# Query projections of a four-layer cross-attention kernel: one fp32 matmul against three bf16 products

## The reference, cut to what matters

```python
x      # (32, 56, 128)
ctx    # (32, 1500, 64)
# every layer, for each of 16 heads:
q = norm(x) @ Wq ; k = ctx @ Wk ; v = ctx @ Wv
x = x + softmax(q k^T * scale) v @ Wo
x = x + ffn(norm(x))       # experts, int8-like product, Fourier product, self-attention + MLPs
```

## Time and profile before

| | |
|---|---|
| median of three runs | 4396.57 us (4387.61 to 4402.43) |
| profiled execution, its span | 4385.4 us |
| what lies around the span, to the median | 11.17 us |
| TensorE busy | 4003.2 us, 91% |
| vector engine busy | 3408.8 us, 78% |
| scalar engine busy | 2756.6 us, 63% |
| GpSimd busy | 2685.0 us, 61% |
| mean granted TensorE clock | 0.939 |

### The profile page before, as it was taken

One profiled execution on the slowest core, in us unless ns is written; L12 is line 12 of the kernel. 1 busy time (PEld: TensorE's weight loads), 2 busy tenths in 40 slices (PEclk: granted clock), 3 DMA queues, 4 the chain that ended last, 5 costly groups with the idle time before them and its releaser, 6 DMA issues. The chain is left out here.

```text
span 4385.4 us, 103422 instructions
## 1 busy us (share of the span) xinstructions
PE 4003.2 (91%) x40427; PEld 2873.2 (66%) x40427; DVE 3408.8 (78%) x6672; ACT 2756.6 (63%) x5342; POOL 2685.0 (61%) x2445
## 2 busy tenths in 40 slices
PE   6999999888879999999799999996996899999977
PEld 4777777754545777777467777774664577777753
DVE  6999998667788888888688888876555888888833
ACT  4787877554446777777377777761441677777721
POOL 3888888656664767777367677771002476767730
PEclk9999999889989999999699999995997999999986
DMA  4333333124341111111111111100001111111100
GB/s 112 94 90 96 87 99 89 53 62 119 117 118 43 51 40 51 49 46 30 33 41 46 53 37 54 44 23 19 1 1 32 45 46 46 46 54 42 34 12 9
DMA packets 113025, 237.08 MB, mean 54 GB/s; under 512 B 15000, under 2 KB 53160, under 8 KB 111160
## 3 DMA queue, kind: packets, MB, share of 16 engines
q1 hardware_dynamic: 112088, 230.40, 18.3%
q10 hardware_dynamic: 448, 0.06, 0.0%
HBM read 165.23 MB, written 50.26 MB: 49 GB/s over the span
## 5 line engine op out<-in xcount | busy, mean ns | idle before, releaser
L483 POOL TENSOR_TENSOR wst<-wst 125x384 bf16<-125x384 f32 (+1 forms) x1536 | 1631.5, 1062 | 841.3 <-ACT wst L681 776.7
L681 ACT ACTIVATE wst<-ps 125x448 f32<-125x448 f32 x3072 | 1498.1, 543 | 406.9 <-PE ps L164 397.9
L738 DVE TENSOR_TENSOR wst<-wst 125x512 bf16<-125x512 f32 (+1 forms) x1536 | 1403.9, 915 | 270.5 <-ACT wst L681 254.9
L164 PE MATMUL ps<-big,cx 128*125 128x448 bf16 (+1 forms) x6144 | 1435.1, 355 | 0.0
L164 PEld LDWEIGHTS ps<-cx,wst 125*128 125x128 bf16 x23040 | 1105.4, 98 | 354.7 <-issue 60.2
L164 PE MATMUL ps<-cx,wst 125*128 125x65 bf16 (+2 forms) x23040 | 1202.3, 204 | 27.8 <-POOL wst L483 13.3
L164 PEld LDWEIGHTS ps<-big,cx 128*125 128x125 bf16 (+1 forms) x6144 | 814.6, 137 | 287.2 <-issue 23.1
L164 PE MATMUL ps<-cx,big 128*128 128x500 bf16 (+1 forms) x2688 | 713.2, 318 | 27.7 <-DVE wst L708 14.2
L705 DVE CUSTOM_DVE_ANT_0 wst<-ps,wst 128x500 bf16<-128x500 f32 x896 | 603.8, 674 | 166.3 <-PE ps L164 122.5
L630 ACT ACTIVATE wst<-ps 128x500 bf16<-128x500 f32 x896 | 530.1, 592 | 226.9 <-PE ps L164 173.5
L708 DVE TENSOR_REDUCE wst<-ps 128x1 f32<-128x500 f32 x896 | 600.5, 670 | 36.3 <-PE ps L164 27.1
(11 more groups left out here) (213 smaller groups left out, 4158.2 us busy)
## 6 DMA issues: line engine op xcount, KB each, us to landing
cx<-ctxT SPq DMA_DIRECT2D x96, 375.0 KB, 3.5
cx<-ctxN SPq DMA_DIRECT2D x64, 377.9 KB
cx<-in_ctxN SPq DMA_DIRECT2D x64, 375.0 KB
cx<-ctxT SPq DMA_DIRECT2D x96, 187.5 KB, 3.8
ctxN<-cx SPq DMA_DIRECT2D x32, 377.9 KB
ynN<-cx SPq DMA_DIRECT2D x32, 377.9 KB
cx<-ynN SPq DMA_DIRECT2D x32, 377.9 KB
cTs<-in_ctxT SPq DMA_DIRECT2D x64, 187.5 KB, 6.8
```

The source lines that it names most:

```text
L164: return t.matmul(o, l, r, start=start, stop=stop, skip_group_check=True)
L483: g.tensor_tensor(pl[r][0:KP, at:], pf[r][0:KP, at:], pf[r][0:KP, at:].bitcast(BF16)[:, 1::2], ALU.subtract).then_inc(s["plp"], 1)
L681: e.activation(pf[T % 3][0:KP, cols], bank(2 + n2 % 3, 448)[0:KP], ACT.Exp, scale=scale).then_inc(s["ev"], 1)
L738: v.tensor_tensor(pl[r][0:KP, 0:to], pf[r][0:KP, 0:to], pf[r][0:KP, 0:to].bitcast(BF16)[:, 1::2], ALU.subtract).then_inc(s["pl"], 1)
```

## The change

The projection becomes a sum of three bf16 products. Both operands are written as an upper bf16 half and the bf16 remainder: `xTh` and `xTl` in place of the turned activations, `wah` and `wal` beside the folded weights. The product of the two remainders is left out.

```diff
+            def project(o, g, c):
+                mm(t, o, wah2[:, g, :], tok8(xh_, c), True, False)
+                mm(t, o, wah2[:, g, :], tok8(xl_, c), False, False)
+                mm(t, o, wal2[:, g, :], tok8(xh_, c), False, True).then_inc(s["pm"], 1)
...
-                mm(t, bank((1 + g) % 8, 448), wa2[:, g, :], tok8(qsrc, 0), True, True).then_inc(s["pm"], 1)
+                project(bank((1 + g) % 8, 448), g, 0)
...
-                    mm(t, bank(7, 448), wa2[:, k, :], tok8(qsrc, p), True, True).then_inc(s["pm"], 1)
+                    project(bank(7, 448), k, p)
```

```diff
+        def act_turned_high(e, w, n):
+            for g4 in range(4):
+                w.wait_ge(s["tr"], 4 * n + g4 + 1)
+                e.activation(xTh[:, 512 * g4:512 * g4 + 512], bank(g4), ACT.Copy).then_inc(s["xTa"], 1)
+
+        def dve_turned_low(v, w, n):
+            for g4 in range(4):
+                cols = slice(512 * g4, 512 * g4 + 512)
+                w.wait_ge(s["xTa"], TURNED[n] - 3 + g4)
+                v.tensor_tensor(xTl[:, cols], bank(g4), xTh[:, cols], ALU.subtract).then_inc(s["xTd"], 1)
```

The folded weights. In layer 0 the scalar engine writes `wah` from PSUM and the vector engine `wal` from PSUM. In layers 1 and 2 the scalar engine writes `wa` and `wah`, and GpSimd subtracts. In the last layer (fold 4) both halves are made from `wa`, and the turned activations get theirs from `xT`:

```diff
+                if f == 4:
+                    w.wait_ge(s["f1d"], FOLD_D[3] + j + 1)
+                    e.activation(wah[:, 512 * j:512 * j + 512], wa[:, 512 * j:512 * j + 512], ACT.Copy).then_inc(s["f1a"], 1)
+                    continue
...
+                if f != 3:
+                    e.activation(wah[:, 512 * j:512 * j + 512], bank(4 + j), ACT.Copy).then_inc(s["f1a"], 1)
...
+        def pool_weights_low(g, w, f):
+            for j in range(2):
+                cols = slice(512 * j, 512 * j + 512)
+                w.wait_ge(s["f1a"], FOLD_A[f])
+                g.tensor_tensor(wal[:, cols], wa[:, cols], wah[:, cols], ALU.subtract).then_inc(s["wl"], 1)
+                w.wait_ge(s["wl"], FOLD_W[f] - 1 + j)
...
+            for g4 in range(4):
+                cols = slice(512 * g4, 512 * g4 + 512)
+                w.wait_ge(s["x3h"], g4 + 1)
+                g.tensor_tensor(x3l[:, cols], xT[:, cols], x3h[:, cols], ALU.subtract).then_inc(s["x3l"], 1)
+                w.wait_ge(s["x3l"], g4 + 1)
+            pool_weights_low(g, w, 4)
...
+            for g4 in range(4):
+                cols = slice(512 * g4, 512 * g4 + 512)
+                w.wait_ge(s["xTf"], 13 + g4)
+                e.activation(x3h[:, cols], xT[:, cols], ACT.Copy).then_inc(s["x3h"], 1)
```

More of the change, by code:

```diff
@@ L73, in build @@
         wav = wa[:, :].rearrange("p (h n) -> p h n", h=H)
-        wa2 = wa[:, 0:1024].rearrange("p (g n) -> p g n", g=H // 2)
+        wah, wal = (wa[:, 1024 + 512 * i:1536 + 512 * i].bitcast(BF16) for i in range(2))
+        wah2, wal2 = (v.rearrange("p (g n) -> p g n", g=H // 2) for v in (wah, wal))
+        xTh, xTl = (xT[:, 1024 * i:1024 * i + 1024].bitcast(BF16) for i in range(2))
         wbh = wb[:, 0:1024].bitcast(BF16)
@@ L192, in wait_turned @@
         def wait_turned(w, n):
-            w.wait_ge(s["xTd"], 2 * n + 2)
-            w.wait_ge(s["xTa"], 2 * n + 2)
+            w.wait_ge(s["xTd"], TURNED[n])
+            w.wait_ge(s["xTa"], TURNED[n])
         jobs1 = (0, 2, 4, 6, 10)
@@ L222, in pe_fold @@
                 r.then_inc(s["f2"], 1)
+        CLEAR_A1, CLEAR_MLP, CLEAR_F4 = 2, 4, 8
         EARLY = (1, 2)
-        FOLD_A = (1, 3, 5, 7, 7)
-        FOLD_D = (1, 1, 1, 3, 5)
+        FOLD_A = (2, 6, 10, 12, 14)
+        FOLD_D = (0, 0, 0, 2, 4)
+        FOLD_W = (2, 4, 6, 6, 8)
         FOLD_HI = (8, 24, 40, 44, 52)
@@ L243, in dve_fold @@
                                 lyg.unsqueeze(1).broadcast_to([128, per, C]), ALU.mult).then_inc(s["f1d"], 1)
-            for j in range(0, 0 if f == 4 else H // per, 2):
+            for j in range(2 if f == 0 else 0):
+                cols = slice(512 * j, 512 * j + 512)
+                w.wait_ge(s["f1a"], j + 1)
+                v.tensor_tensor(wal[:, cols], bank(4 + j), wah[:, cols], ALU.subtract).then_inc(s["wl"], 1)
+            for j in range(0, H // per if f == 3 else 0, 2):
                 w.wait_ge(s["f1"], jobs1[f] + j + 1)
@@ L261, in act_fold @@
             per, copies = 512 // n, 128 // n
-            for j in range(0 if f in EARLY else 1, 0 if f == 4 else H // per, 1 if f in EARLY else 2):
-                w.wait_ge(s["f1"], jobs1[f] + j + 1)
-                e.activation(fold_out(n)[:, per * j:per * j + per, :],
-                             bank(4 + j).rearrange("p (h c) -> p h c", c=n), ACT.Copy).then_inc(s["f1a"], 1)
+            for j in range(1 if f == 3 else 0, H // per, 2 if f == 3 else 1):
+                if f == 4:
+                    w.wait_ge(s["f1d"], FOLD_D[3] + j + 1)
+                    e.activation(wah[:, 512 * j:512 * j + 512], wa[:, 512 * j:512 * j + 512], ACT.Copy).then_inc(s["f1a"], 1)
+                    continue
+                w.wait_ge(s["f1"], jobs1[f] + j + 1)
+                if f != 0:
+                    e.activation(fold_out(n)[:, per * j:per * j + per, :],
+                                 bank(4 + j).rearrange("p (h c) -> p h c", c=n), ACT.Copy).then_inc(s["f1a"], 1)
+                if f != 3:
+                    e.activation(wah[:, 512 * j:512 * j + 512], bank(4 + j), ACT.Copy).then_inc(s["f1a"], 1)
             for j in range(4):
@@ L278, in act_fold @@
                     e.activation(w32[n * r:n * r + n, cols], bank(k)[0:n, :], ACT.Copy).then_inc(s["f2a"], 1)
+        def pool_weights_low(g, w, f):
+            for j in range(2):
+                cols = slice(512 * j, 512 * j + 512)
+                w.wait_ge(s["f1a"], FOLD_A[f])
+                g.tensor_tensor(wal[:, cols], wa[:, cols], wah[:, cols], ALU.subtract).then_inc(s["wl"], 1)
+                w.wait_ge(s["wl"], FOLD_W[f] - 1 + j)
         def pool_fold(g, w, f):
+            pool_weights_low(g, w, f)
             for j in range(4):
@@ L799, in dve_l0 @@
             dve_norm(v, w, 0, x, xn)
-            dve_turned(v, w, 0, xT)
+            dve_turned_low(v, w, 0)
             dve_fold(v, w, 0, 64)
         def act_l0(e, w):
-            act_turned(e, w, 0, xT)
+            act_turned_high(e, w, 0)
             act_high(e, w, 0)
@@ L934, in pool_f0 @@
             for i, o in enumerate(oo):
-                g.memset(o, 0.0).then_inc(s["oz"], 1)
-                w.wait_ge(s["oz"], i + 1)
+                g.memset(o, 0.0).then_inc(s["clear"], 1)
+                w.wait_ge(s["clear"], i + 1)
             pool_norm(g, w, 1)
@@ L1733, in wait_mlp @@
             w.wait_ge(s["hd"], NP * (i + 1))
+        x3h, x3l = (cTs[:, 1024 * i:1024 * i + 1024].bitcast(BF16) for i in range(2))
         def sp_a2(y, w):
@@ L1764, in pe_a2 @@
             wait_folded(w, 4)
-            w.wait_ge(s["xTf"], 16)
+            w.wait_ge(s["x3h"], 4)
+            w.wait_ge(s["x3l"], 4)
         def dve_a2(v, w):
@@ L1946, in _ @@
             pe_l0(t, w)
-            pe_cross(t, w, 0, xT)
+            pe_cross(t, w, 0, xTh, xTl)
             pe_f0(t, w)
             pe_l1(t, w)
-            pe_cross(t, w, 1, xT)
+            pe_cross(t, w, 1, xTh, xTl)
             pe_f1(t, w)
             pe_l2(t, w)
-            pe_cross(t, w, 2, xT)
+            pe_cross(t, w, 2, xTh, xTl)
             pe_f2(t, w)
@@ L1958, in _ @@
             pe_a2(t, w)
[L1959 removed]
+            pe_cross(t, w, 3, x3h, x3l)
             wait_cross(w, 3)
```

37 lines of the change are left out of this document (19 added, 18 removed), and 8 rows, old and new, of the table s.

## The result

The changed kernel takes 4360.94 us, median of four executions (4358.80 to 4363.98), against 4396.80 us of before, run beside it (4387.61 to 4402.43): ratio 0.9918, 95% interval 0.9904 to 0.9932. The forecast of 4377.1 us was 16 us too high, and its range, from 4367, did not hold it. Direction and mechanism were right. What failed was the size: the forecast added 11.17 us to the span as if they were fixed, and it counted 19.5 us of saving where the traces show 24.9.

The account below looks back on a forecast made before the run. It took TensorE to bound the loops, the vector engine close behind. Span 4385.4 less 19.5 us for the loops, with 0.0 for the heads, gave 4365.9; plus 11.2 to the median made 4377.1 us, range 4367 to 4392.

Parts of the forecast that it names:

- The loops: Context loops of layers 1 to 3: TensorE sets the pace, 72 projections gain 0.23 us each, 16.6 us.
- exposed load: At each loop projection, the first weight load may not be hidden: 0.03 us, making 0.60 us with three matmuls.
- The first loop: First context loop: the vector engine has 640 columns per tile and lets only part of the gain pass, 2.9 us.
- The third place: Behind a block's third projection in the first loop: 0.14 us of free vector engine time, gained 6 times.
- The heads: Work ahead of the loops in all four layers: costs and gains sum to 0.0 us, ends -2 and +10.
- the term of layer 1: Head of layer 1: four subtractions replace two copies, 1.6 us more, less 0.19 for the projection; cost 1.4 us.
- Nothing at the least, if the transfers were held by others anyway: Head of layer 1: lower end of its cost, if other things already held the transfers of `Qh`.
- Layers 0 and 3: Heads of the first and last layer: shorter projections let splits start earlier, gains of 0.8 and 0.7 us.
- The step from the span to the median: Whole kernel: the median lies 11.17 us above the profiled span, so 4365.9 + 11.2 = 4377.1 us.
- The vector engine as the bound of all loops: Rival, all four loops: the vector engine takes over, gain only 11.6 us, 4385 us; chance 0.22.
- Heads that eat the gain: Rival, heads: late GpSimd, unrelieved turning and longer 1.2 GHz stretches lose 19.2 us, 4396 us; chance 0.08.
- Exposed loads: Rival, 96 loop projections: three loads exposed between matmuls, 0.90 us against 0.83, 4406 us; chance 0.07.

Follow-up runs that it names:

- with extra matmuls: 80 idle bf16 matmuls behind the ranking's matmuls of the last part, added to before (4394.89 us, ratio 0.9992) and to after (4368.31 us, 0.9948).
- the cut kernels: Before and after, each without its last feed-forward part: 4256.03 us and 4231.68 us.
- delayed: After with four fills of 2048 columns on the vector engine ahead of the last feed-forward part: 4377.87 us, ratio 0.9963 to before.
- before with 512 columns: Before with 512 instead of 640 columns of lower halves on the vector engine in the first loop: 4385.25 us; the same in after: 4360.27 us.
- the kernel with only the halves: After with all halves written, but every projection again one fp32 matmul over the same bytes: 4399.24 us, ratio 1.0029 to before.
- the kernel with one product: After with only the upper-by-upper product of the three in each projection: 4342.09 us, ratio 0.9883 to before.

## Why the prediction was wrong

Stages by trace, mean of the four traces of before (two, with extra matmuls, cut) and the five of after (two, with extra matmuls, delayed, cut), each worked out from starts of rows ("normalization" here starts with its statistics, 4.9 us ahead of the first row with `xn` in layers 1 and 2):

```
us                                           before    after   change  forecast
loops, first to last projection, 4 layers    1982.1   1961.3    -20.9     -19.5
layer 0, first projection to first product     14.4     13.1     -1.2      -0.8
layer 1, normalization to first product        28.8     28.3     -0.5      +1.4
layer 2, the same                              28.1     28.3     +0.2      +0.1
layer 3, normalization to first product        45.6     43.5     -2.1      -0.7
first product to the loop's first projection   86.4     85.4     -1.0         0
after the last projection, 4 layers          1119.7   1119.0     -0.7         0
```

Of the last layer's -2.1 us, 1.3 lie ahead of the projections, where before takes 29.7 us in two traces and 32.9 in two, by the clock, and after 30.0; 0.8 are the projections'. In two kernels made from after, it is 33.1 too. Without the 1.3 the sum is 24.9 us; the cut kernels say 24.35, closer than their few executions allow, which is in part luck. The table leaves out what lies ahead of layer 0's projections, the feed-forward parts and the last part. Of these the feed-forward part of layer 0 (normalization to layer 1's normalization) took 432.1 to 432.6 us in the traces of before and 429.9 to 430.8 in those of after; as it took 430.2 us in before with 512 columns and 433.8 in after with them, it is not counted as a saving.

**The loops: right in mechanism, 1.4 us too small with the first one.** TensorE sets the pace of layers 1 to 3, and the gain comes through (6.5, 5.5 and 5.5 us a loop by the means). The 0.03 us taken for an exposed load do not exist: the three loads of 128 rows lie wholly beneath the matmuls. That settles the place where the Trainium skill (TensorE: Matmul & The Clock Gate, section The mechanism) was weighed: its strict rule on row groups would have given 0.90 us or so, the trace shows 0.57, as its sentence on the background buffer has it. This term was 17.5 instead of 16.6 us.

**The first loop: right in size, partly wrong in its working.** 3.4 us against 2.9. The third place, forecast with 0.14 us each, gives nothing: the vector engine's 0.14 us of free time was not on TensorE's path. What makes up for it is the loop's entry, at half clock, where a projection's distance falls from 1.49 to between 0.76 and 1.12 us. The block fell by 0.28 us, not 0.4, and the wait for the vector engine did not grow.

**The heads: the term of layer 1 was mis-sized.** Its projections come 1.2 us later (1.6 were taken), the scalar engine's first split 0.9 us (1.4 were forecast), and the issue of the copies of `Qh` 0.9 us. Yet the first product, which waits for these copies, comes 28.3 us after the normalization where it was 28.8 in the mean. It comes 7.2 to 8.7 us behind the issue in the four traces of before and 6.3 to 7.2 in the five of after. "Nothing at the least, if the transfers were held by others anyway" was the end that held; that other transfers held them is likely, as the kernel with only the halves issues them 17.98 us after the normalization and waits only 3.5 us, but it was not tested. Layers 0 and 3 gained 0.5 us more than forecast. Heads in all -2.3 us, forecast 0.0. GpSimd was never late.

**The step from the span to the median: wrong, and the largest.** "The median lies 11.17 us above the span of the profiled execution" was taken for a constant. What lies around the span is 1.7 to 1.9 us; the other 9.4 were the draw. The profiled execution of before had its last part in 131.2 us, 8 us quicker than the second trace of before and both of after, and two of the three executions timed beside it were from the slow half of a scatter of 20 us. After scatters less: its median lies 3.9 us above its profiled span, so this term alone was 7.2 us too large.

The miss of 16.1 us comes apart like this. The change's own saving was 5.4 us larger than forecast (24.9 against 19.5: loops 1.4, heads 2.3, the stretches around the loops 1.7), and 7.2 are the step to the median. The other 3.5 are what differs by the draw between the two profiled spans (4385.4 and 4357.0, 28.4 apart, of which 24.9 are the change): after's last part was 8.1 us longer, and about 11.6 us were won elsewhere, among them 3.2 ahead of layer 0's projections (39.5 against 36.2), 2.8 between the last layer's normalization and its projections (32.9 against 30.1) and 2.2 in the feed-forward part of layer 0. Had the forecast started from the median of before's twelve executions (4388.37), it would have been 4368.9 us, still 8 us too high.

**The rivals.** The vector engine as the bound of all loops: ruled out, by the 0.3 us of idle time left behind each projection and by the kernel with one product. Heads that eat the gain: ruled out by the table. Exposed loads: ruled out by the 0.57 us. What stays open is why before and after draw their half-clock stretches differently; the kernel with a delay of 9 us scatters otherwise than after, but by which rule no run shows.

A version that is surely better than after was not found: with 512 columns in the first loop its quickest execution (4354.21) is the quickest seen of the whole computation, but the medians are the same (4360.27 against 4360.51).

## What to carry to other kernels

Before adding a "rest" to a profiled span, look at how single executions lie to their own spans; if the median of a few is far from the profile, the distance is scatter, and belongs in the range and not in the sum. Where a stage ends in a part that runs at either level of the clock, measure a change with that part taken out: the same saving was read as 36 and as 28 us from whole kernels, with a scatter of 20 us in one of them, and as 24 us with a scatter of 5. In a loop that the matmuls hold, a projection's price is nearly what TensorE spends on it. Do not take the next engine's idle time behind it for the limit: in the last loop three projections showed idle times of 0.30, 0.56 and 0.29 us, 1.15 together, and the block fell by 0.79 us and then, with one product, by another 0.94.

## What the runs showed of the hardware

- Three bf16 matmuls with 448 columns and their loads of 128 rows take 0.57 us at 2.4 GHz, one fp32 matmul of the same shape 0.83 us.
- Extra matmuls ahead of the last part's work did not keep its clock high: 80 in a row ran at 1.2 GHz at first and then for over 15 us at 2.4 GHz, TensorE idled for 4.21 us, and from the pair behind the next transposes on the work ran at 1.2 GHz, where without the 80 it had begun at 2.4 GHz. This was seen in one trace.
- The 288 matmuls of the last part took 92 or 100 us in two executions of one kernel, and 108 us in a kernel changed only elsewhere, at mean granted clocks of 0.62, 0.56 and 0.53.
- The time around the span is 1.7 to 1.9 us in all executions on record with their span, and 2.2 in the changed kernel cut short.
